# Two experts per sample in groups of two sizes, and token splitting moved from before the copy to after it

## The reference

```python
gate_logits = gate_in @ gate_w + gate_b          # one row per sample, 4 experts
gate_logits = gate_logits * (1.0 + scale) + shift
topk_w, topk_i = jax.lax.top_k(jax.nn.softmax(gate_logits), 2)
...
for e in range(4):
    h = gelu(context_c @ ew1[e] + eb1[e])        # 128 -> 512
    y = h @ ew2[e] + eb2[e]                      # 512 -> 128
    out = out + w_be[:, e][:, None, None] * mask[e][None, :, None] * y
shared = gelu(context_c @ sw1 + sb1) @ sw2 + sb2
return out + shared
```

## Time and profile before

| | us |
|---|---|
| median of 3 runs | 905.42 |
| lowest and highest run | 903.06, 905.49 |
| profiled execution, run time | 902.24 |
| profiled execution, span | 900.1 |

### The profile page before, as it was taken

How to read it: one execution, slowest core, us unless ns; L and a number is a source line. 1 busy time by engine, 2 the same in 40 slices (tenths; PEclk the granted TensorE clock), 3 DMA queues, 4 the chain that set the end, 5 groups by cost and what they waited for, 6 DMA issues and landing times.

```text
span 900.1 us, 12449 instructions
## 1 busy us (share of the span) xinstructions
PE 878.9 (98%) x3830; PEld 699.0 (78%) x3830; DVE 688.3 (76%) x1072; ACT 574.5 (64%) x997; POOL 391.0 (43%) x363
## 2 busy tenths in 40 slices
PE   8999999999999999999999999999999999999996
PEld 5778788887888888888888888888888777777773
DVE  7767777778788787676686686686676887998887
ACT  6777677865555455555555555555555678989896
POOL 7424544124455453243343342352322226754465
PEclk9999999999999999999999999999999999999999
DMA  9599994023023111012012012011010048171630
GB/s 306 187 286 308 318 292 155 1 86 132 0 63 125 52 48 75 8 48 83 1 47 83 1 47 82 1 48 48 0 48 1 1 89 195 36 179 49 163 106 35
DMA packets 36401, 86.15 MB, mean 96 GB/s; under 512 B 4464, under 2 KB 15472, under 8 KB 34416
## 3 DMA queue, kind: packets, MB, share of 16 engines
q1 hardware_dynamic: 36336, 85.37, 30.5%
HBM read 68.84 MB, written 6.83 MB: 84 GB/s over the span
## 4 chain that ended last, share of the span: by engine, by line
PE 83%; DVE 7%; ACT 3%; issue 3%; DMA 3%; POOL 1%; SPq 0%; DVEq 0%; ACTq 0%
PE ps L842 17%; PE ps L859 17%; PE ps L847 17%; PE ps L889 9%; PE ps L896 9%; PE ps L894 9%; DVE HL L1405 2%; DMA CWB<-scratch 2%; PE ps L876 2%; PE ps L874 1%; ACT HH L975 1%; DVE HH L1402 1%; DVE Hf L1393 1%; PE ps L762 1%; DVE Hf L1386 1%
## 5 line engine op out<-in xcount | busy, mean ns | idle before, releaser
L969 ACT ACTIVATE Sg<-ps 128x512 f32<-128x512 f32 x288 | 171.8, 598 | 244.5 <-PE ps L859 244.2
L1386 DVE TENSOR_TENSOR Hf<-ps,Sg 128x512 f32<-128x512 f32 x288 | 197.9, 688 | 147.8 <-ACT Sg L969 98.4
L1477 POOL TENSOR_TENSOR HL<-Hf,HH 128x512 fp32r<-128x512 f32 x136 | 182.3, 1347 | 168.4 <-ACT HH L975 151.8
L975 ACT ACTIVATE HH<-Hf 128x512 fp32r<-128x512 f32 x346 | 216.2, 625 | 21.4 <-DVE Hf L1386 13.3
L1405 DVE TENSOR_TENSOR HL<-Hf,HH 128x512 fp32r<-128x512 f32 x242 | 214.5, 887 | 4.3 <-ACT HH L975 3.2
L842 PE MATMUL ps<-XHL,WBH 128*128 128x512 f32 x512 | 203.3, 397 | 1.2 <-DVE Hf L1386 1.2
L859 PE MATMUL ps<-XHL,WBH 128*128 128x512 f32 x512 | 202.1, 395 | 0.0
L847 PE MATMUL ps<-XHL,WBL 128*128 128x512 f32 x512 | 201.6, 394 | 0.0
L1492 POOL TENSOR_TENSOR XT<-XT,TMP 128x512 f32<-128x512 f32 x64 | 83.5, 1305 | 250.2 <-DVE TMP L1282 250.2
L842 PEld LDWEIGHTS ps<-XHL,WBH 128*128 128x128 f32 x512 | 96.1, 188 | 23.9 <-DVE Hf L1386 2.3
L859 PEld LDWEIGHTS ps<-XHL,WBH 128*128 128x128 f32 x512 | 96.2, 188 | 22.5
(11 more groups left out here) (245 smaller groups left out, 1318.8 us busy)
## 6 DMA issues: line engine op xcount, KB each, us to landing
CWB<-scratch SPq DMA_DIRECT2D x68, 256.0 KB, 7.3
CWB<-scratch SPq DMA_DIRECT2D x15, 1024.0 KB, 4.7
GWD<-expert_down SPq DMA_DIRECT2D x19, 576.5 KB, 5.8
GWU<-expert_up SPq DMA_DIRECT2D x19, 514.0 KB, 5.1
GX<-XHL SPq DMA_DIRECT2D x76, 128.0 KB, 3.9
ST<-in_wb_dram SPq DMA_DIRECT2D x8, 768.0 KB, 6.5
XT<-in_x_dram SPq DMA_DIRECT2D x8, 256.0 KB, 5.6
expert_up<-GWU SPq DMA_DIRECT2D x4, 512.0 KB, 4.6
```

Source lines behind the costliest of these rows:

```text
L969: e.activation(Sg[:, it.n % NG, :], zb[z % NZ][:, :], ACT.Silu).then_inc(s_act, 1)
L975: e.activation(HH[:, it.n % NH, 0:it.cols], hidden_place(it), ACT.Copy).then_inc(s_hi_act, 1)
L1386: e.tensor_tensor(Hf[:, it.n % NS, :], zb[z % NZ][:, :], Sg[:, it.n % NG, :], ALU.mult).then_inc(s_prod, 1)
L1477: e.tensor_tensor(HL[:, it.n % NH, :], Hf[:, it.n % NS, :], HH[:, it.n % NH, :].bitcast(F32), ALU.subtract).then_inc(s_lo_pool, 1)
```

## The change

Samples of an expert are packed into two kinds of group: 13 full ones of four (512 columns) and 8 halves of two (256 columns), 21 groups and 68 places in all. Per expert, three or four remaining pairs fill a full group; smaller rests, and what does not fit in the 13, go to halves. The order of the groups is fixed by a string of F and H. The arithmetic of the places at `g_key` is longer for it, and so is the constant that it compares with.

Tokens are no longer kept split by sample. A copy brings the plain fp32 tokens of a sample (512 B per partition) from XT into GX (now one plane), and on chip ScalarE copies them to the high part of a new tile GHL (two buffers) and GpSimd subtracts for the low part, at slot (g - 1, f = 1) for group g (`split_g`). The first up matmul of a group waits for the high part (s_g_hi), its third for the low part (s_g_lo). The loads no longer wait for the split blocks of x; `load_x` moves to slot (g - 3, f = 1) and is parted from `load_u`. The split of blocks 6 and 7 moves from slots 8 and 12 into groups 2 and 6. XHL is written and read without the per-sample view.

```diff
+FULL, HALVES = 13, 8
+NGRP = FULL + HALVES
+NPAIR = 4 * FULL + 2 * HALVES
+def group_order():
+    full = [(4 * i, 4, i) for i in range(FULL)]
+    half = [(4 * FULL + 2 * i, 2, FULL + i) for i in range(HALVES)]
+    return [(full if c == "F" else half).pop(0) for c in "HFFFHFHFFHFHFFHFFHFFH"]
...
-        self.cols = BLK
+        self.cols = GROUPS[blk][1] * P if kind == "G" else BLK
...
-        GX = sb("GX", [P, NR, 4, 2, P], F32R, actx)
+        GX = sb("GX", [P, NR, BLK], F32, actx)
+        GHL = sb("GHL", [P, 2, 2, BLK], F32R, actx)
...
-        split_end = {8: 6, 12: 7}
+        split_end = {pos["G", 2, 0, 0].k: (6, 0), pos["G", 2, 0, 2].k: (6, 1), pos["G", 6, 0, 0].k: (7, 0),
+                     pos["G", 6, 0, 2].k: (7, 1)}
+        split_g = {pos["G", g - 1, 0, 1].k if g else pos["G", 0, 0, 0].k - 1: g for g in range(NGRP)}
...
-        load_x = {pos["G", g - NR, 0, 3].k + 1: g for g in range(NR, NGRP)}
+        load_x = {pos["G", g - NR, 0, 1].k: g for g in range(NR, NGRP)}
+        load_u = {pos["G", g - NR, 0, 3].k + 1: g for g in range(NR, NGRP)}
...
                 if k == first_load:
-                    e.wait_ge(s_x_hi, NBLK - 2)
-                    e.wait_ge(s_x_lo, NBLK - 3)
-                    e.wait_ge(s_x_end, 4)
+                    for b in range(NBLK):
+                        e.wait_ge(f_x[b], 16)
...
         def load_tokens(e, g, v):
-            for j in range(4):
-                e.dma_start(GX[:, g % NR, j, :, :].bitcast(F32).rearrange("p a t -> p (a t)"),
-                            XS[:, bass.ds(v[j], 1), :, :].bitcast(F32).rearrange("p s a t -> p (s a t)")).then_inc(
-                                f_gx[g % NR], 16)
+            for j in range(GROUPS[g][1]):
+                e.dma_start(GX[:, g % NR, j * P:j * P + P],
+                            XSAMPLE[:, bass.ds(v[j], 1), :].rearrange("p s t -> p (s t)")).then_inc(f_gx[g % NR], 16)
...
                 if it.kind == "G" and it.f == 0:
-                    e.wait_ge(f_gx[it.blk % NR], 64 * (it.blk // NR + 1))
+                    e.wait_ge(s_g_hi, it.blk + 1)
...
+                if fresh and it.kind == "G":
+                    e.wait_ge(s_g_lo, it.blk + 1)
...
(ScalarE)
+                if k in split_g:
+                    g = split_g[k]
+                    c = slice(0, GROUPS[g][1] * P)
+                    e.wait_ge(*tokens_loaded(g))
+                    if g >= 2:
+                        e.wait_ge(s_z, pos["G", g - 2, 0, 3].z[0] + 1)
+                    e.activation(GHL[:, g % 2, 0, c], GX[:, g % NR, c], ACT.Copy).then_inc(s_g_hi, 1)
...
(VectorE, slot g_key: seven linked operations become 17, among them, twice)
+                    def before(out, number):
+                        wide = bc(bc(number, 1, [NB, 5, 4]), 3, shape)
+                        link(e.tensor_tensor(more, wide, upto, ALU.is_gt))
+                        after()
+                        link(e.tensor_reduce(out, more.rearrange("p a e j -> p a (e j)"), AX, ALU.add))
+                        after()
...
(GpSimd)
+                if k in split_g:
+                    g = split_g[k]
+                    c = slice(0, GROUPS[g][1] * P)
+                    e.wait_ge(*tokens_loaded(g))
+                    e.wait_ge(s_g_hi, g + 1)
+                    e.tensor_tensor(GHL[:, g % 2, 1, c], GX[:, g % NR, c], GHL[:, g % 2, 0, c].bitcast(F32),
+                                    ALU.subtract).then_inc(s_g_lo, 1)
...
-                        for j in range(4):
+                        for j in range(GROUPS[it.blk][1]):
```

More of the change, by code:

```diff
@@ L384, in acc_done @@
         def acc_done(t):
-            return s_acc, 4 * (t + 1) if t < NGRP else 3 * NGRP + t + 1
+            return s_acc, sum(GROUPS[g][1] for g in range(min(t + 1, NGRP))) + max(0, t + 1 - NGRP)
         def acc_a(b):
@@ L527, in tokens, with tokens_loaded @@
         def tokens(it, part):
-            if it.kind == "G":
-                return GX[:, it.blk % NR, :, part, :]
-            return XS[:, 4 * it.blk:4 * it.blk + 4, part, :] if it.kind == "A" else XHL[:, it.blk, part, :]
+            return GHL[:, it.blk % 2, part, 0:it.cols] if it.kind == "G" else XHL[:, it.blk, part, :]
+        def tokens_loaded(g):
+            return f_gx[g % NR], 16 * sum(GROUPS[i][1] for i in range(g % NR, g + 1, NR))
         def up_weights(it, j):
@@ L688, in indices @@
             _, v = nc.values_load_multi_w_load_instructions(
-                index[0:1, g, a:b], engines=(engine,), min_val=0, max_val=most,
+                index[0:1, GROUPS[g][2], a:b], engines=(engine,), min_val=0, max_val=most,
                 skip_runtime_bounds_check_because="the table counts 32 samples and 4 experts and is clamped")
@@ L1073, in gates @@
+                    odd, left, low, at2, end = [v(i) for i in (24, 25, 26, 27, 28)]
+                    def before(out, number):
[4 more added lines that the diff above has]
+                        after()
+                    e.wait_ge(f_sm2, 16)
                     e.wait_ge(*small.of("sort"))
-                    link(e.tensor_tensor(more, bc(bj[0:NB, 260:264], 2, [NB, 4, 8]),
-                                         S("four")[0:NB, :].rearrange("p (e j) -> p e j", j=8), ALU.is_gt))
+                    before(fours, count)
@@ L1087, in gates @@
                                                 op1=ALU.add))
                     after()
-                    link(e.tensor_tensor(key, v(21), sel, ALU.mult))
+                    link(e.scalar_tensor_tensor(out=left, in0=most, scalar=-8.0, in1=odd, op0=ALU.mult, op1=ALU.add))
+                    link(e.scalar_tensor_tensor(out=end, in0=most, scalar=4.0, in1=rank, op0=ALU.mult, op1=ALU.is_ge))
+                    link(e.scalar_tensor_tensor(out=low, in0=most, scalar=-4.0, in1=rank, op0=ALU.mult, op1=ALU.add))
@@ new lines, in gates @@
+                    after()
+                    before(twos, left)
+                    link(e.scalar_tensor_tensor(out=at2, in0=twos[:, 0:4], scalar=2.0, in1=low, op0=ALU.mult, op1=ALU.add))
+                    after()
+                    link(e.scalar_tensor_tensor(out=at4, in0=at4, scalar=float(4 * FULL), in1=at2, op0=ALU.subtract,
+                                                op1=ALU.subtract))
+                    after()
+                    link(e.tensor_tensor(at4, at4, end, ALU.mult))
@@ L1090, in gates @@
+                    after()
+                    link(e.scalar_tensor_tensor(out=key, in0=at2, scalar=float(4 * FULL), in1=at4, op0=ALU.add,
+                                                op1=ALU.add))
+                    after()
+                    link(e.tensor_tensor(key, key, sel, ALU.mult))
                 if k == g_pairs:
@@ L1268, in finish @@
                 if it.kind == "G":
+                    n = it.cols
                     if it.blk == 0:
```

142 lines of the change are left out of this document (75 added, 67 removed).

## The result

The kernel after takes 917.27 us (median of four runs, 916.59 to 918.68); the kernel before 904.24 us (four runs, 902.20 to 905.49). The ratio is 1.0148 with a 95% interval of 1.0122 to 1.0174. The change costs 13.0 us; the forecast was 8.3.

The account below looks back on a forecast made before the run. TensorE bounds the kernel (98% busy, 83% of the last chain); -9.4 + 13.6 + 1.3 + 2.8 = +8.3 us gives 910.5 on the profiled execution, 913.7 as median; own range 909 to 918, wider range 900 to 920.

Parts of the forecast that it names:

- Matmuls, -9.4: TensorE's grouped matmuls: 105.8 us fall to 96.4, with 256-column matmuls 0.125 us apart; gain 9.4 us.
- half the columns are not half the time: Rival: weight load not hidden behind 256 columns, spacing 0.19 to 0.232; 13 to 18 us more, 918 to 923; chance 0.08.
- bound of 11.9 at 0.11: Grouped matmuls: the gain if 256-column matmuls came every 0.11 us, the floor read from 16-column ones.
- The chain that ends on GpSimd, +13.6: Grouped stage: the low-part subtraction, appended behind GpSimd's accumulations, makes TensorE's third up matmul wait; 13.6 us in all.
- the prediction's kinds: Groups sorted by the full or half groups before them, each kind with its own matmul time, chain and wait, 0.33 to 1.40.
- half-width prices by slopes: Chain links of half groups, priced from full and small forms on each engine: subtraction 0.68, accumulations 0.86 us.
- GpSimd hands over sooner: Rival: chain 1.0 us shorter at every group, waits fall to 2.3 us; total 901.1; chance 0.15.
- Weight splits, +1.3: Three GpSimd subtractions for second-stage weights around group 10, no longer hidden by slack; 1.3 us (0 to 2.6).
- SyncE's queue and the transfers, 0: Grouped stage: 99 us of SyncE work against 107, and 27.3 instead of 30.4 MB moved; costed at zero.
- The start, +2.8: Before the first groups: longer key arithmetic delays index and loads; 2.8 us (1 to 4.5), TensorE's key wait zero.
- the prediction's chain of loads: First four groups: third up matmuls at 46.3, 52.2, 57.3 and 62.7, set by token issue and landing.
- Behind the groups, 0: Everything behind the grouped stage is TensorE's and untouched; no cost.

Follow-up runs that it names:

- early: Kernel after with each group's token split one slot earlier on ScalarE and GpSimd, ahead of the accumulations; 903.21 us, ratio 0.9999 to before.
- split_only: Kernel before's 19 full groups and its key arithmetic, with only the tokens split on chip, in after's slot; 917.06 us, ratio 1.0164 to before.
- early_port_key12: Kernel after with the split one slot earlier, the key's intermediate room in PSUM, and sort and key at slot 12; 898.61 us, ratio 0.9949 to before.
- busy: Kernel after plus twenty useless matmuls on TensorE in front of its wait for the pairs; 916.14 us, ratio 1.0148 to before.
- key_only: Kernel after with the key arithmetic at slot 13 and the routing steps behind it one slot earlier; 917.40 us, ratio 1.0150 to before.
- halves_port_key12: Kernel after with tokens split beforehand as in before, room in PSUM, and sort and key at slot 12; 900.83 us, ratio 0.9981 to before.
- port: Kernel after with the key's intermediate room in PSUM and full computed from it; 914.97 us, ratio 1.0142 to before.

## Why the prediction was right and where it failed

The 16.8 us between the two profiled executions, by the milestones, beside the prediction's terms: start of the first group +7.2 (forecast 1.9, from the third up matmul at 46.3 instead of 44.4); first to last up product +6.5 (forecast 8.0: the waits 13.6, the weight splits 1.3, 0.9 left of the start, less 7.8 of the matmuls, whose other 1.6 fall behind it); from there to the second mixture -1.7 (forecast -1.6); second mixture +1.7 and the rest +3.1 (forecast 0). The forecast's terms add to 8.3, the measured ones to 16.8. The medians differ by only 13.0, since the profiled execution of after was the slowest of its four, 1.4 us above their median, and that of before 2.0 us below its own.

**Matmuls, -9.4: right.** TensorE's timeline of after shows the 256-column matmuls 0.12 us apart, 0.118 on the average of 176 pairs (forecast 0.125, between 0.11 and 0.232), which makes it -10.7; the first two start at 51.12 and 51.24. So the weight load adds nothing to 256 columns either, and the rival "half the columns are not half the time" falls. (The bound of 11.9 at 0.11 was added up wrong: 105.8 - 72.4 - 21.1 is 12.3.)

**The chain that ends on GpSimd, +13.6: right, in sum and almost group by group.** The booked wait for the low part is 13.3 us in 12 times; 1.4 of that belongs to the weight splits below, and 0.16 per wait has to be added for the distance of starts. That leaves 13.8 us for the chain. TensorE's third up matmuls with their booked waits, by the prediction's kinds:

```profile
82.90 0.39 PE L882 MATMUL ps<-GHL,GWU 128*128 128x256 f32 x1 [0.68 <-POOL GHL L1539]
...
88.20 0.50 PE L882 MATMUL ps<-GHL,GWU 128*128 128x512 f32 x1 [0.94 <-POOL GHL L1539]
...
94.01 0.50 PE L882 MATMUL ps<-GHL,GWU 128*128 128x512 f32 x1 [1.03 <-POOL GHL L1539]
```

By starts, a full behind a half that follows two fulls waits 1.40, 1.43 and 1.43 (forecast 1.40), the second full 1.19, 1.17, 1.17 and 1.16 (1.18), half, full, half 0.84 (0.85), and the full behind it 1.10 and 0.66 (0.62). Group 4, for which 0.33 was forecast, is not in the list. The half-width prices by slopes held: the subtraction took 0.70 to 0.74 us (0.68), two accumulations 0.88 (0.86), WM 0.61. early and split_only show that the waits were the cause and not only a sign. The links of the full chain were added up 0.03 us too long, which changes nothing. The rival "GpSimd hands over sooner" would have needed 0.7 us less.

**Weight splits, +1.3: right in kind, small.** Group 10 waits 1.69 as booked, about 0.4 more than its like, and group 11 waits 0.82 (for HL) and 1.64, where 0.68 would be due: 2.4 us together by starts, within the 0 to 2.6 given.

**SyncE's queue and the transfers, 0: right.** The DMA share fell to 0.81 and the tokens landed 2.4 us after their issue (3.9 before; 3.5 had been taken for them). In early_port_key12 the groups take 101.8 us, and TensorE has no listed wait for a load there.

**The start, +2.8: wrong, and this is the step that failed.** The prediction added it up along the loads, from the issue to the landing of the tokens, and said: "What TensorE waits longer for the key in the routing part falls before the first group, whose start the loads set anyway: zero." The loads set it neither before nor after. TensorE reached the first group without a wait, 7.2 us later, and the delay has three pieces. The longer chain was there as forecast, 1.9 us. To it came 2.3 us because three of the new operations were held by GpSimd: the durations of the earlier trace rows came from operations with an operand in PSUM, and were carried over to some that had none there. The row of an operation's shape is not its price if the operands lie elsewhere. The third piece is the clock: TensorE was idle for 4.8 us, the granted clock fell, and the matmuls behind the wait ran at the low level, 3.2 us, and 3.3 in busy. (The pieces add to 7.4; the key began 0.2 us sooner.) The Trainium skill, page "TensorE: Matmul & The Clock Gate", section "What's actually happening", says that the slow level is the default and activity lifts it. The trace agrees (0.50 behind the idle time, 1.00 once the matmuls had run for a while), and the prediction had used that page only for the spacing. Nor did the loads set the pace of the next groups: from the first group to the fourth it is 14.3 us, what the prediction had for the matmuls alone (14.36), where the prediction's chain of loads gave 16.4. In the prediction's own terms the start cost 6.2 us: the fourth group's third up matmul is at 65.94 instead of 62.27, and 2.5 us of matmuls were saved by then.

**Behind the groups, 0: wrong,** by 4.8 us in the profiled execution. "Everything behind the grouped stage is TensorE's and is untouched" holds for the program, not for the time.

So the sum that was forecast as -9.4 + 13.6 + 1.3 + 2.8 measures -10.7 + 13.8 + 2.4 + 6.2, and + 4.8 behind the groups: 16.5 of the 16.8 us. What is left is small. Behind each of the 13 waits the next matmul comes 0.1 us late, and before has a stall of 1.2 us in front of a down product at 104.23, for which its profile names no cause and which after lacks.

The time fell into the range (900 to 920) and at the upper edge of the forecast's own (909 to 918). The core of the forecast, the 13.6, was right. That the time came so near is in part luck: two misses of 3.4 (the start) and 4.8 us (behind the groups) were damped, by 1.3 more saved by the matmuls and above all because the two medians lie 3.8 us closer together than the two profiled spans.

## What to carry to other kernels

An operation that somebody waits for must not be appended to a chain that was off the critical path only because nobody waited for its end: lay the engines' timelines over one period and put it into that engine's idle time, here one slot earlier for some 14 us. A few tiny operations in front of a wait of TensorE cost more than their length, since they may be held by the neighbour engine's instruction and since a wait of 4.8 us lowered the clock for the work behind it. Whether loads set the start of a stage is read from TensorE's timeline: here its matmuls came at an even distance, so nothing in front of the stage was free. Two parts that gain nothing alone (halves, 903.27; split one slot forward, 904.95) can hide a gain that shows in full only with both and with the front in order: 898.61.

## What the runs showed of the hardware

- VectorE on 32x4 with all operands in SBUF took up to 1.24 us beside a GpSimd instruction on SBUF (1.04, 0.63 and 1.23 in after, 1.24, 0.15 and 0.38 in early), and 0.14 to 0.15 with an operand in PSUM. The second of the three is a TENSOR_SCALAR with a single tensor input. It was held in after, where it began behind the start of a GpSimd CAST, and not in early, where both began at 31.22.
- A wait of TensorE of 4.8 us, and also those of 3.7 (early), 3.0 (key_only), 2.7 (halves_port_key12) and 2.5 (port), was followed by a granted clock of 0.50 in a stretch of 2 us; in busy a wait of 1.65 us that came 0.5 us behind one of 0.78 was, and the same pair in after was not.
- A booked wait of TensorE was 0.16 us shorter than the delay by starts, for 256 and for 512 columns, since it counts from the modelled end of the matmul before it.
- The 0.3% between 547.1 and 548.9 us in a stage of unchanged code, in every kernel with halves and in none without, is the size of many effects one would like to measure; it stays without a cause.
